# A graph layer, linear attention and a mixture of experts on one core: the attention of all tiles moved into the first thirteen steps

## The reference

```python
xn = layernorm(x)
# graph layer: mean over the incoming edges of a projected source row
Wh = xn @ W + b
h = segment_sum(Wh[src], dst) / maximum(degree, 1)
# linear attention over all nodes, 8 heads of 32; feature map elu(z) + 1
q, k, v = fmap(xn @ wq + bq), fmap(xn @ wk + bk), xn @ wv + bv
kv, k_sum = einsum('bshd,bshe->bhde', k, v), k.sum(1)
mix = (q @ kv / (q @ k_sum + 1e-6)) @ wo + bo
x = x + h + mix
# mixture of 8 experts: top one, at most 977 rows each
y = layernorm(x); e = argmax(softmax(y @ gate_w + gate_b))
x = x + p[e] * (relu(y @ w1[e] + b1[e]) @ w2[e] + b2[e])   # kept rows only
```

## Time and profile before

| what | us |
|---|---|
| median of the runs | 1489.97 |
| the profiled execution's own time | 1488.93 |
| its span, first to last instruction | 1487.2 |
| PE busy | 1086.4 (73%) |
| POOL busy | 916.3 (62%) |
| DVE busy | 817.5 (55%) |
| ACT busy | 550.0 (37%) |

### The profile page before, as it was taken

One profiled execution on the slowest core, in us unless ns is written; L12 is line 12 of the kernel. 1 busy time (PEld: TensorE's weight loads), 2 busy tenths in 40 slices (PEclk: granted clock), 3 DMA queues, 4 the chain that ended last, 5 costly groups with the idle time before them and its releaser, 6 DMA issues.

```text
span 1487.2 us, 32776 instructions
## 1 busy us (share of the span) xinstructions
PE 1086.4 (73%) x5569; PEld 754.3 (51%) x5570; DVE 817.5 (55%) x2765; ACT 550.0 (37%) x1458; POOL 916.3 (62%) x967
## 2 busy tenths in 40 slices
PE   2669877455445547677878787888888888888896
PEld 2346544122122215445646566666666656666885
DVE  5954432232244434556657676777777677777443
ACT  2832211011021123334434444545444555455342
POOL 3546777777777776777677776667667657611111
PEclk9999996565576777899899999999999999999998
DMA  7484333443444464555455554555655545534452
GB/s 244 146 242 138 104 104 105 132 135 108 131 137 132 141 191 142 143 174 184 135 177 179 174 169 151 179 171 174 188 180 187 186 156 181 160 105 130 149 179 88
DMA packets 143360, 231.62 MB, mean 156 GB/s; under 512 B 29824, under 2 KB 87329, under 8 KB 143248
## 3 DMA queue, kind: packets, MB, share of 16 engines
q0 software_dynamic: 42896, 115.65, 26.0%
q1 hardware_dynamic: 99118, 114.27, 24.7%
q10 hardware_dynamic: 1234, 0.66, 0.2%
HBM read 197.40 MB, written 35.08 MB: 156 GB/s over the span
## 4 chain that ended last, share of the span: by engine, by line
issue 27%; POOL 24%; DVE 18%; PE 13%; DVEq 6%; DMA 4%; POOLq 3%; ACT 3%; SPq 1%; ACTq 0%; PEldq 0%
POOL shared L570 24%; PE pY L977 4%; PE pH L986 3%; DVE shared L1355 3%; PE pA L888 2%; DMA shared<-table,idx 2%; DVEq L1310 1%; DMA shared<-in_L_ffn_b_dram 1%; DVEq L1305 1%; PE pH L868 1%; DVE shared L1457 1%; DVE shared L1464 1%; DVE stats L1396 1%; DVE shared L1469 1%; DVE shared L1357 1%
## 5 line engine op out<-in xcount | busy, mean ns | idle before, releaser
L570 POOL DMA_INDIRECT shared<-table,idx x784 | 764.1, 975 | 313.0 <-issue 270.7
L888 PE MATMUL pA<-shared,onehot 128*128 x976 | 322.3, 444 | 274.0 <-POOLq L550 190.2
L888 PEld LDWEIGHTS pA<-shared,onehot 128*128 x976 | 98.5, 101 | 485.6 <-issue 415.0
L1297 DVE TENSOR_TENSOR onehot<-tile_iota,dst_t 128x512 f32 x244 | 160.1, 695 | 159.4 <-PE pA L888 125.2
L977 PE MATMUL pY<-w2s,shared 128*128 x864 | 201.6, 388 | 7.5 <-issue 4.5
L986 PEld LDWEIGHTS pH<-shared 128*128 128x128 f32 x1728 | 201.4, 192 | 2.7
L986 PE MATMUL pH<-shared 128*128 128x128 f32 x1728 | 201.7, 275 | 0.0
L977 PEld LDWEIGHTS pY<-w2s,shared 128*128 128x128 f32 x864 | 163.8, 195 | 30.0 <-issue 9.1
L680 ACT ACTIVATE shared<-pA,rdeg 128x256 f32<-128x256 f32 x49 | 23.2, 473 | 406.0 <-DVE rdeg L1367 406.0
L737 ACT ACTIVATE shared<-pH,b1s 128x128 f32<-128x128 f32 x432 | 120.4, 374 | 67.1 <-PE pH L986 55.6
L510 POOL DMA_INDIRECT out_dram<-shared,jtok x54 | 55.1, 1020 | 110.7 <-issue 110.7
(11 more groups left out here) (245 smaller groups left out, 1501.8 us busy)
## 6 DMA issues: line engine op xcount, KB each, us to landing
shared<-in_L_ffn_w_dram SPq DMA_DIRECT2D x108, 512.0 KB
shared<-table,idx POOLq DMA_INDIRECT x784
w2s<-in_L_ffn_w_dram SPq DMA_DIRECT2D x8, 1024.0 KB, 6.5
rows<-rows_sb SPq DMA_DIRECT2D x7, 1040.0 KB, 15.0
shared<-rows SPq DMA_DIRECT2D x54, 130.0 KB
shared<-in_L_ffn_b_dram SPq DMA_DIRECT2D x54, 128.0 KB
shared<-in_x_dram SPq DMA_DIRECT2D x12, 512.0 KB, 8.7
table<-w2s SPq DMA_DIRECT2D x12, 512.0 KB, 3.0
```

Of the source, the lines that this page charges most:

```text
L570: g.indirect_dma_start(gathered[:, s * G + j, :], None, table[:, :], bass.IndirectOffsetOnAxis(ap=idx[:, q * G + j:q * G + j + 1], axis=0) ...
L888: m = pe.matmul(pA[:, :], onehot[:, n % OQ, j, :], gathered[:, (f % RQ) * G + j, :], start=False, stop=final and j == G - 1)
L1297: v.tensor_tensor(onehot[:, n % OQ, :, :], tile_iota[:, :].rearrange("p (a n) -> p a n", a=1).broadcast_to([P, G, P]), dst_t[:, bass.ds(ch ...
```

## The change

The attention of a tile becomes a *tick* of its own, and the 50 ticks (tile i's scaling and tile i-1's product with `ms`; the last one only the product) are dealt out to the first thirteen steps: 8, 7, 5, 5, 4, 4, 4, 3, 2, 2, 2, 2, 2. In a step all its ticks stand as one block: on PE between the clearing of `pA` and the next tile's sums, on DVE and ACT at the step's end, on SP as a loop of `xres` loads. A tile's attention plus its residual is kept in `base`, which takes the place of that tile's turned x in `xts`; `node_out` reads it. `bo` comes in by a one-row matmul.

The sums are no longer scaled when they leave `pA`: ACT copies both halves (`ss`, 512 wide), PE joins the halves while it turns them (four real matmuls, with an identity and one divided by `LO`, in place of two transposes), and `node_out` multiplies by 1/degree. `combine`, `residual` and `tb` go. To make room, `src_t` is held in 16 bits and `post` keeps its mask in a buffer of its own and waits for `fin_free` ahead of it. The first thirteen steps are written out instead of looped.

```diff
+TICKS_OF = (8, 7, 5, 5, 4, 4, 4, 3, 2, 2, 2, 2, 2)
+TICK0 = [sum(TICKS_OF[:t]) for t in range(len(TICKS_OF) + 1)]
+ATT = len(TICKS_OF)
...
+            def load_res(i, last=False):
+
+                sp.wait_ge(S["xo_ok"], i)
                 hold(sp, "sp_hold")
                 if last:
                     sp.dma_start(xres[0:LAST, :], x[(NT - 1) * P:N, :]).then_inc(S["xr_in"], 16)
                 else:
-                    sp.dma_start(xres, x_t[bass.ds(t, 1), :, :].rearrange("t p d -> p (t d)")).then_inc(S["xr_in"], 16)
+                    sp.dma_start(xres, x_t[bass.ds(i, 1), :, :].rearrange("t p d -> p (t d)")).then_inc(S["xr_in"], 16)
+
+            def load_res_of(t):
+
+                lo, hi = max(TICK0[t], 1), min(TICK0[t + 1], NT - 1)
+                if lo < hi:
+                    with sp.Fori(lo, hi) as i:
+                        load_res(i)
+                if TICK0[t] <= NT - 1 < TICK0[t + 1]:
+                    load_res(NT - 1, True)
 
             def store_x1(t, last=False):
 
...
                 if bias:
                     load_bias(t - T0, bias == "first")
                 if big:
                     load_out(t)
+                if isinstance(t, int) and t < ATT:
+                    load_res_of(t)
                 if not isinstance(t, int) or 1 <= t <= NT:
                     stored(t - 1)
...
             def ready(t):
 
-                a.wait_ge(S["rdeg_ok"], t + 1)
+                a.wait_ge(S["agg_done"], t + 1)
                 a.sem_inc(S["act_hold"], 1)
-                a.activation(ss, pA[:, 0:D], ACT.Copy, scale=rdeg[:, 0:1]).then_inc(S["ah_ok"], 1)
-
-            def query(t, den=True):
-
-                if isinstance(t, int) and t == 0:
-                    a.wait_ge(S["qd_ps"], 1)
-                else:
-                    a.wait_ge(S["qf_ok"], t)
+                if not isinstance(t, int) or t > 0:
+                    a.wait_ge(S["rdeg_ok"], t)
                     a.sem_inc(S["act_hold"], 1)
-                    a.wait_ge(S["qd_ps"], t + 1)
+                a.activation(ss, pA[:, :], ACT.Copy).then_inc(S["ah_ok"], 1)
+
+            def query(i):
+
+                a.wait_ge(S["q_ps"], i + 1)
+                a.sem_inc(S["act_hold"], 1)
                 for out_, f in ((qr, ACT.Relu), (qe, ACT.Exp)):
                     for k in range(DK):
                         ins = a.activation(out_[:, k * P:(k + 1) * P], pQ[:, k * P:(k + 1) * P], f, bias=bqs[:, k:k + 1])
                 ins.then_inc(S["qe_ok"], 1)
 
-            def divisor(t):
-
-                a.wait_ge(S["qd_ps"], t + 2)
-                a.activation(qn, pQ[:, D:2 * D], ACT.Identity, bias=eps[:, 1:2]).then_inc(S["dn_ok"], 1)
+            def tick(i):
+
+                a.wait_ge(S["d_ps"], i + 1)
+                a.sem_inc(S["act_hold"], 1)
+                a.activation(dn, pT[:, 0:D], ACT.Identity, bias=eps[:, 1:2]).then_inc(S["dn_ok"], 1)
+                if not isinstance(i, int) or i + 1 < NT:
+                    query(i + 1)
+
+            def ticks_of(t):
+
+                lo, hi = TICK0[t], min(TICK0[t + 1], NT - 1)
+                if lo < hi:
+                    with a.Fori(lo, hi) as i:
+                        tick(i)
+                if lo <= NT - 1 < TICK0[t + 1]:
+                    tick(NT - 1)
...
-                def query(t):
+                def query(i):
 
                     for m in range(DK):
                         for k in range(DK):
                             ins = pe.matmul(pQ[:, m * P:(m + 1) * P], wqs[:, k, m * P:(m + 1) * P],
-                                            xts[:, bass.ds(t, 1), k, :].rearrange("p t n -> p (t n)"),
+                                            xts[:, bass.ds(i, 1), k, :].rearrange("p t n -> p (t n)"),
                                             start=(k == 0), stop=(k == DK - 1))
-                    return ins
-
-                def divisor(t):
+                    ins.then_inc(S["q_ps"], 1)
+
+                def divisor():
 
                     for m in range(DK):
-                        ins = pe.matmul(pQ[:, D + m * P:D + (m + 1) * P], ks[:, m, :], qf[:, m * P:(m + 1) * P], start=True, stop=True)
-                    return ins
+                        ins = pe.matmul(pT[:, m * P:(m + 1) * P], ks[:, m, :], qf[:, m * P:(m + 1) * P], start=True, stop=True)
+                    ins.then_inc(S["d_ps"], 1)
+
+                def attend():
+
+                    for m in range(DK):
+                        pe.matmul(pD[:, 0:GW], qn[:, m * P:(m + 1) * P], ms[:, m, :], start=(m == 0), stop=False)
+                    pe.matmul(pD[:, 0:D], tri[0:1, :], bob[0:1, :], start=False, stop=True).then_inc(S["o_ps"], 1)
+
+                def tick(i):
+
+                    inner = not isinstance(i, int)
+                    if inner or i < NT:
+                        pe.wait_ge(S["qf_ok"], i + 1)
+                        pe.sem_inc(S["pe_hold"], 1)
+                        divisor()
+                    if inner or i + 1 < NT:
+                        query(i + 1)
+                    if inner or i >= 2:
+                        pe.wait_ge(S["xo_ok"], i - 1)
+                        pe.sem_inc(S["pe_hold"], 1)
+                    if not inner and i == NT:
+                        pe.wait_ge(S["qn_ok"], NT)
+                    if inner or i >= 1:
+                        attend()
+
+                def ticks_of(t):
+
+                    pe.wait_ge(S["t_sb"], t + 1)
+                    for i in range(TICK0[t], min(TICK0[t + 1], 2)):
+                        tick(i)
+                    lo, hi = max(TICK0[t], 2), min(TICK0[t + 1], NT - 1)
+                    if lo < hi:
+                        with pe.Fori(lo, hi) as i:
+                            tick(i)
+                    for i in range(max(TICK0[t], NT - 1), TICK0[t + 1]):
+                        tick(i)
 
                 def project_sum(t):
 
                     pe.wait_ge(S["t_sb"], t + 1)
                     pe.sem_inc(S["pe_hold"], 1)
-                    pe.wait_ge(S["qn_ok"], t + 1)
                     if not isinstance(t, int) or t >= 1:
-                        pe.sem_inc(S["pe_hold"], 1)
                         pe.wait_ge(S["px_free"], t)
-                    pe.matmul(pX[:, 0:GW], st[:, 0:P], wgs[:, 0, :], start=True, stop=False)
-                    pe.matmul(pX[:, 0:GW], st[:, P:D], wgs[:, 1, :], start=False, stop=False)
-                    for m in range(DK):
-                        ins = pe.matmul(pX[:, 0:GW], qn[:, m * P:(m + 1) * P], ms[:, m, :], start=False, stop=(m == DK - 1))
+                    for k in range(DK):
+                        ins = pe.matmul(pX[:, 0:GW], st[:, k * P:(k + 1) * P], wgs[:, k, :], start=(k == 0), stop=(k == DK - 1))
                     return ins
 
                 def count(t):
 
...
                 def turn_sums(t):
 
-                    pe.wait_ge(S["s_ok"], t + 1)
+                    pe.wait_ge(S["ah_ok"], t + 1)
                     pe.sem_inc(S["pe_hold"], 1)
+                    if isinstance(t, int) and 1 <= t <= ATT:
+                        pe.wait_ge(S["dn_ok"], min(TICK0[t], NT))
                     for k in range(DK):
-                        ins = pe.transpose(pT[:, k * P:(k + 1) * P], ss[:, k * P:(k + 1) * P], ident[:, :])
+                        pe.matmul(pT[:, k * P:(k + 1) * P], ss[:, k * P:(k + 1) * P], ident[:, :], start=True, stop=False)
+                        ins = pe.matmul(pT[:, k * P:(k + 1) * P], ss[:, D + k * P:D + (k + 1) * P], ident_lo[:, :], start=False, stop=True)
                     return ins
...
                         ins = count(t - 2)
                     if inner or t >= 1:
                         ins.then_inc(S["px_ps"], 1)
-                    if inner or t < NT:
-                        pe.wait_ge(S["qf_ok"], t + 1)
-                        pe.sem_inc(S["pe_hold"], 1)
-                        if inner or t + 1 < NT:
-                            query(t + 1)
-                        divisor(t).then_inc(S["qd_ps"], 1)
...
                     ins.then_inc(S["t_ps"], 1)
                     if inner or t + 1 < NT:
                         sum_start(load_span(t + 1))
+                        if not inner and t < ATT:
+                            ticks_of(t)
                         sum_rest()
 
...
                 def next_tile(t):
 
                     load_ends(t + 1)
+                    v.wait_ge(S["agg_done"], t + 1)
+                    v.sem_inc(S["dve_hold"], 1)
                     v.wait_ge(S["oh_ready"], v.snap(pair_r))
                     v.sem_inc(S["dve_hold"], 1)
...
-                def queries(t):
-
-                    if not isinstance(t, int) or t > 0:
-                        v.wait_ge(S["qn_ok"], t)
+                def queries(i):
+
+                    if not isinstance(i, int) or i >= 1:
+                        v.wait_ge(S["qn_ok"], i)
                         hold(v, "dve_hold")
-                    v.wait_ge(S["qe_ok"], t + 1)
```

(141 more changed lines are left out.)

32 lines of the change are left out of this document (13 added, 19 removed).

## The result

The changed kernel takes 1555.63 us (median, 1547.07 to 1559.78) against 1490.81 of the kernel before on the same chip: the ratio is 1.0433 [1.0379, 1.0488], slower, as forecast, though by 65 us where 1528 meant 38. The profiled execution took 1559.12 us with a span of 1557.3.

The account below looks back on a forecast made before the run. The prediction took POOL to bound the early stage and PE the late one. Own time 1488.9 + 112 early - 72 late = 1529, median 1 us above, stated as 1528 us; range 1472 to 1592, the forecast's own 1495 to 1560.

Parts of the forecast that it names:

- the stage: From the end of tile 0's sums to that of tile 13's: 537 us for 425.6, 112 us more.
- slow rival: Ticks at PE's lower clock or behind slow loads: 6.0 us a tick, 65 us more, 1593; chance 0.18.
- The tick, 4.7 us: Time per tick in a block, taken from the xres load loop; 50 ticks make 235 us, bounds 4.4 to 6.0.
- My chain of 4.5: Serial links of a tick: divisor, ACT's copy, reciprocal, product, feature sum, gap and hand-overs, 4.5 us.
- The bound of 6.0: Upper bound in us of a tick: PE at 1.2 GHz, the product waiting for PE's four matmul groups.
- The load loop: Single-buffered xres beside the tick's chain: result, SyncE's issue and a 3.9 us load make 4.7 us.
- The fixed parts: Work around the ticks between old and new sums in the thirteen blocks: 124 us in all.
- The rounds, 161 + 17 us: Early stage's 89 rounds of sums at 1.81 us, plus 17 us lost to POOL's full ring in tiles 1 to 3.
- The delay of tile 1: Tile 1's twelve rounds, the last four waiting for late gathers: 32.9 us where PE alone needs 21.7.
- The late gain, 72 us: Late steps fall from 11.2 to 9.6 us plus rounds, saving 72 us; bounds 45 and 115.
- The first late window: 693.8:927.7, 233.9 us before, ends at POOL's pace, about 213; the second, 927.7:1337.7, takes 360 for 410.
- the fast rival: Cheap block, late stage at POOL's floor: early 84 us more, late gain 115 or 100, 1458 or 1473; chance 0.18.

Follow-up runs that it names:

- x2: Changed kernel with four useless 128x512 matmuls on PE ahead of each tick's wait for the feature sum: 1510.74 us, ratio 1.0181.
- x3: Changed kernel without the one-row matmul that adds bo in each tick (bo missing from the output): 1518.48 us, ratio 1.0204.
- x6: Changed kernel with each tick's reciprocal replaced by a multiplication by one, attention left unscaled: 1522.67 us, ratio 1.0237.
- x8: Changed kernel with a round of sums after each tick and five one-hot buffers instead of four: 1460.82 us, ratio 0.9817.
- x5: Changed kernel with SyncE issuing a job's weights ahead of the next job's rows in every step: 1539.23 us, ratio 1.034.

## Why the prediction was right, and where its terms were off

**Slower, and where.** The mechanism held: blocks stop PE's sums, POOL fills its ring and stands still (27.2 and 25.3 us in the first two blocks, "about 20" forecast, and 6 to 13 us in each of the next six), and the early loss is larger than the late gain. Tile 13's sums end at 803.2 (795 forecast) and the stage is 541 (537). That it is so near is luck: gaps and ticks took 33 us more than forecast, the rounds 29 less. Had the rounds taken their 178, the time would have been some 1585 (an estimate: 1555.6 + 29), outside the forecast's own 1495 to 1560 and close to the 1593 of its slow rival. The sum itself has a slip that decides nothing: 1529 of the execution and 1 us more make 1530, not 1528.

**The tick, 4.7 us, was mis-sized: 5.79.** Over 36 pairs in blocks that makes 39 us. My chain of 4.5 was nearly right at the higher clock (x2: 4.66), but I had set its PE links from rows at that clock (four loads of the divisor's weights in 0.53 us, 0.52 in x2, but 0.93 at 356.59 of the changed kernel). The bound of 6.0, and the rival to which I gave 0.18, named what happened: the product waits for PE's four matmul groups. x3, x2 and x6 show it from three sides. My argument against that rival was the clock of the late windows, where PE hardly waits; a block has the pauses of a chain, and the earlier trace rows with 0.56 was the nearer row. The Trainium skill (TensorE: Matmul & The Clock Gate, HAM oscillation — how this bites in real kernels) tells of a kernel whose waits between bursts of matmuls drop the clock anew in every turn of its loop. The 0.64 here against x2's 0.95 is of that kind, though PE's waits of 1.3 to 1.6 us in most ticks are shorter than the waits of that kernel.

**The load loop was no limit.** I had two loops of about equal length, the chain and `xres`. A residual load was waited for once in the stage, at its very end, and x8's ticks of 4.67 us have one load each. The 3.9 us of the earlier trace rows was too long for this load: in x6 one is issued at 637.85 and its reader starts 3.65 us later, right behind DVE's operation before it. That the wrong loop gave 4.7 is luck too.

```profile
637.85 0.36 SPq L365 DMA_DIRECT2D shared<-in_x_dram  x1
...
641.50 0.17 DVE L1429 TENSOR_TENSOR xgs<-pD,xgs 128x8 f32 x1
```

**The fixed parts were near.** The time from a tile's last sum to the next tile's first round is 392.4 us in the thirteen blocks; without the 36 pairs (208) that leaves 184, where the forecast has 124 + 14 x 4.7 = 190.

**The rounds, 161 + 17 us, took 148.6.** The delay of tile 1 is as forecast (32.3 for 32.9). But rounds that wait ready behind a block are faster than the 1.81 us of the earlier trace rows:

```profile
546.84 4.88 PE L915 MATMUL pA<-shared,onehot 128*128 x20
...
552.39 1.14 PE L915 MATMUL pA<-shared,onehot 128*128 x4 [0.67 <-DVE onehot L1354]
554.25 1.11 PE L915 MATMUL pA<-shared,onehot 128*128 x4 [0.72 <-issue]
```

Five rounds in 4.88 us, without the pause of 0.7 us ahead of each.

**The late gain, 72 us, was 42.** The first late window took 223.0 us for 213 forecast, the second 381.3 for 360. Of the missing 30, 7 to 13 are the weights behind the scatter (x5, against x2 and x3 or against the changed kernel). Some 8 may be PE's step, an estimate from one step: from 1260.24 to 1275.60 it takes 15.36 us with three rounds, 15.0 forecast, over the 23 steps of the second window. The rest was not traced to a cause. With x5's order the gain is 55, still under 72. Its first window, 214.7, is at the pace forecast for POOL; its second, 375.9, is far above POOL's 327, so the fast rival's late half is refuted too.

**What the forecast did not see** is that the block's cost lay in its order, not in its place: with a round in each tick the stage costs 9 us more than before (434.3 for 425.6) instead of 115, and the late gain (36 us, 624.8 for 661.1) shows.

## What to carry to other kernels

A serial chain moved to where an engine "has time" gives that engine its pauses too, so price its links at the clock that a pausing PE is granted, and look for independent work to put into the pauses. Where such work is added, count for each buffer which later instruction reports it free: one slot too few can put a whole chain behind it. Where one engine issues loads in order, look at what each waits for: a load that PE needs next should not stand behind one that waits for another engine's scatter.

## What was not expected of the hardware

PE busy for three quarters of a block (34.75 of 46.10 us, with seven pauses of 1.4 to 2.8 us) was granted 0.72, and 0.64 in the next; with four useless 128x512 matmuls a tick (1.04 us) it was granted 0.98 and 0.95. The bias row's matmul has one row of weights instead of 128, and yet its two passes of 256 columns took 1.22 us at the lower clock (361.21), 0.61 each, no less than the 0.49 us of each full pass of 264 columns ahead of it (1.97 us for four at 359.31): by these rows it is paid by its columns, not by its rows.
